# Rounded three-term products for four projections of a perceiver block, w_down loaded late, and a new order of work on every engine

## The chip, the cores and the metric

The kernel runs on one core of a Trainium2 chip. The metric is the device time of one execution in microseconds (us); lower is better. The core has four compute engines that run their own instruction streams and meet only through semaphores: PE (TensorE, matrix products into PSUM), DVE (VectorE), ACT (ScalarE) and POOL (GpSimd). SP (SyncE) issues most DMAs. Each engine works strictly in the order in which its instructions are written, so a wait at the head of a queue holds everything behind it.

## The reference, cut to what matters

One perceiver block on 64 sequences of 64 rows, 256 wide (4096 rows in all), with a context of 256 rows for each sequence:

```python
x = x + xattn(layernorm(x), ctx)      # 16 heads of 16, layernorm of q and k per head, softmax over 256
x = x + attn(layernorm(x))            # causal over 64 rows, extra term with tanh(q), J, tanh(k)
x = x + ffn(layernorm(x))
# in attn:  Q, K, V = n @ Wq.T + bq, n @ Wk.T + bk, n @ Wv.T + bv
# in ffn:   probs = softmax(h @ router_w); the two best of 16 experts (gate/up 256->128, down 128->256)
#           shared  = (silu(h @ shared_gate_w) * (h @ shared_up_w)) @ shared_down_w
```

Everything is f32. The products that the change touches are `n @ [Wq Wk]` (128 rows by 512 columns for each tile), `n @ Wv` (256 columns), `h @ router_w` (16 columns) and `h @ [shared_gate shared_up]` (512 columns), each with an inner size of 256, which is two blocks (KD = 2) of 128.

## The kernel before, in words

The rows are cut into 32 tiles of 128 (two sequences each). The tiles go through a software pipeline: in step s, an engine works on parts of tile s - lag, and the lag of each part is the number in its `on(s, odd, lag, part, ...)` call. Before the change the lags run from 0 to 6, so there are 32 + 6 steps (`LAGS = 6`, line 46), written out one after the other. The order of the parts within a step is written by hand for every engine in its own `step` function: PE from line 712, ACT from line 936, POOL from line 1056, DVE from line 1355, SP from line 417. PSUM banks are shared by lists of uses (`C_USES`, `B_USES`, `S_USES`, `O_USES`, lines 50 to 53): `claim` makes PE wait, before it writes a bank, until the bank's previous use in the list has been read. Ring C has one bank, ring B two (even and odd places of the list), S is the group of four banks used as one, O one bank.

What one step does on PE, with the names that the text uses:

- R0 and R1 (`rough_scores`, line 544): bf16 scores of the cross attention. DVE takes maxima of them (mx, line 1220), MT (`maxima_turned`, line 553) transposes the maxima, and DVE adds them to the query (`shifted`, line 1225).
- C0 and C1 (`scores`, line 565), then ACT's four exponentials (line 863), then PV0 to PV3 (`weighted`, line 582), DVE's `heads_out` (lines 1234 and 1237), X1 (`cross_output`, line 489 into oA), DVE's `cross_residual` (line 1244) and `self_stats` (lines 1141 to 1146), POOL's power (line 1005) and DVE's `self_normalised` (line 1150), which gives x1n.
- NT (transposes x1n, line 484), ACT's copy into x1T (line 815), QK (`self_qk`, x1T times wa_qk) and VP (`self_values`, x1T times wa_v), both by `product` at line 489. DVE's `self_split`, ACT's tanh, TQ and TK (line 608), MIX (line 617), SS (`self_scores`, lines 626 and 634), the softmax, PT0 and PT1 (`probs_turned`, line 649), O0 and O1 (line 663), WO (line 489 with wa_o).
- HT (transposes h), ACT's copy into hT, RT (`route`, hT times w_route), GU (`gate_and_up`, hT times ws_gu), ST, Y (`down`), and CNT (`counts`, lines 689 to 692), from which DVE's `rows_placed` works out where POOL's indirect DMAs scatter the rows (line 1053).
- K0, K1, V0, V1 (`context_product`, line 500): keys and values of the context. These are already three rounded (fp32r) terms: ct by wx_kv, ct by wx_kv_rest, ct_rest by wx_kv, where the rest is what rounding left out. DVE makes ct (`context_split`), POOL ct_rest (`context_rest`, line 1028). XT and Q make the query, KT and QT transpose keys and queries, and ACT copies those out with `keys_in` (two of 2048 columns, lines 877 and 879) and `queries_in`.

`product` issues one f32 matmul for each of the two blocks of 128; an f32 matmul has two MATMUL records in the trace, so an f32 product shows as x4.

After the pipeline the expert phase works through 80 slots of 128 rows: SP loads the rows that were scattered (from `load_slot`, once every scatter has landed and DVE has worked out the slots, `slots_known`), PE multiplies with w_gu (line 783) and w_down (line 799), and POOL scatters the results. Last, SP reads the two expert rows of each token into a ring of eight buffers (`yg`), DVE adds them to the stored base rows, and ACT writes the output. The weights of the experts, w_down among them, are loaded in twelve pieces of 512 KB in steps 6 to 17, and DVE halves w_down at the head of step 34 (line 1358).

## Time and profile before

| | |
|---|---|
| median of 3 runs | 1395.54 us (1392.45 to 1396.56) |
| the profiled execution, its own time | 1382.54 us |
| its span (first to last instruction) | 1380.7 us |
| PE busy | 1240.6 us, 90% of the span |
| DVE, ACT, POOL busy | 984.4, 698.1, 450.4 us |
| mean granted TensorE clock | 0.955 of full speed |
| chain that ended last | PE 82%, DVE 9%, issue 4%, DMA 2% |

The profiled execution ran 13 us below the median of the runs. In the page's 40 slices of 34.5 us, the first two are the fill, some 30 the steady pipeline, two its drain, and the last six the experts and the output. The end of a matmul record is modelled and overlaps the start of the next, so the distance from start to start tells what a group of matmuls costs.

### The profile page before, as it was taken

How to read it: one execution, taken by the hardware profiler on the slowest of the kernel's cores; microseconds unless marked ns; L12 is line 12 of the kernel's file. 1: busy time of each engine (PE TensorE's matmuls, PEld its weight loads, DVE VectorE, ACT ScalarE, POOL GpSimd, SP SyncE). 2: the span in 40 equal slices, each digit the busy share in tenths (PEclk: the TensorE clock that was granted, in tenths of full speed). 3: DMA queues.
4: the chain of work that ended last, by engine and by line, in shares of the span. 5: the costliest groups of instructions: out<-in, count | busy, mean ns of one | idle time of the engine just before them, and what ended most of it. 6: DMA issues, size and time to landing. Idle time of an engine off the chain costs nothing.

```text
span 1380.7 us, 54869 instructions
## 1 busy us (share of the span) xinstructions
PE 1240.6 (90%) x22808; PEld 1024.0 (74%) x22808; DVE 984.4 (71%) x2498; ACT 698.1 (51%) x1377; POOL 450.4 (33%) x436
## 2 busy tenths in 40 slices
PE   3789999999999999999999999999999986699950
PEld 3677878888888878788878787888888864488840
DVE  7458777777777777777777777777777763365547
ACT  1345555555555555555555555555555542255520
POOL 1322333333333333333333333333333222155530
PEclk7789999999999999999999999999999998699985
DMA  4100111111111111103111100111111002586558
GB/s 155 39 21 4 48 49 49 49 49 49 49 49 51 56 44 51 34 30 100 33 34 33 36 29 28 34 33 34 34 38 33 15 14 63 157 245 188 163 188 262
DMA packets 82579, 92.12 MB, mean 67 GB/s; under 512 B 17248, under 2 KB 72544, under 8 KB 82016
## 3 DMA queue, kind: packets, MB, share of 16 engines
q1 hardware_dynamic: 70816, 65.41, 16.4%
q0 software_dynamic: 6912, 19.01, 3.8%
q8 instruction: 185, 3.03, 0.9%
q10 hardware_dynamic: 4608, 4.20, 0.9%
q14 instruction: 58, 0.48, 0.1%
HBM read 61.19 MB, written 33.78 MB: 69 GB/s over the span
## 4 chain that ended last, share of the span: by engine, by line
PE 82%; DVE 9%; issue 4%; DMA 2%; ACT 1%; POOL 1%; SPq 0%; DVEq 0%; POOLq 0%; ACTq 0%
PE ringB L489 16%; PE ringC L500 14%; PE oA L582 10%; PE banksS L565 9%; DVE mx L1220 6%; PE banksS L783 5%; PE banksS L529 4%; PE ringB L663 3%; PE ringB L617 2%; PE ringB L649 2%; PE banksS L634 2%; PE ringB L484 2%; DMA out<-ksq 2%; PE oA L489 2%; PE banksS L544 2%
## 5 line engine op out<-in xcount | busy, mean ns | idle before, releaser
L863 ACT ACTIVATE pt<-banksS 128x1024 f32<-128x1024 f32 x128 | 127.7, 1023 | 129.6 <-PE banksS L565 118.0
L1039 POOL TENSOR_TENSOR kn<-kc,rr 128x512 f32<-128x512 f32 x64 | 66.6, 1062 | 336.0 <-DVE rr L1208 336.0
L500 PE MATMUL ringC<-wx_kv,ct 128*128 128x256 f32 x512 | 159.9, 312 | 13.6 <-DVE ws_down L1362 6.2
L1220 DVE TENSOR_REDUCE mx<-banksS 128x8 f32<-128x2048 f32 x64 | 146.3, 2287 | 0.9 <-PE banksS L544 0.9
L500 PE MATMUL ringC<-wx_kv_rest,ct 128*128 128x256 f32 x512 | 146.8, 287 | 0.0
L500 PE MATMUL ringC<-wx_kv,ct_rest 128*128 128x256 f32 x512 | 146.0, 285 | 0.0
L1033 POOL TENSOR_TENSOR sc<-sc,rz 128x1024 f32<-128x1024 f32 x32 | 62.3, 1948 | 223.5 <-DVE rz L1281 223.5
L565 PE MATMUL banksS<-qT,kT 17*128 17x64 f32 x4096 | 132.4, 278 | 0.9 <-DVE qT L1225 0.9
L565 PEld LDWEIGHTS banksS<-qT,kT 17*128 17x128 f32 x4096 | 123.5, 191 | 7.9 <-issue 1.4
L500 PEld LDWEIGHTS ringC<-wx_kv,ct 128*128 128x128 f32 x512 | 99.3, 194 | 27.6 <-DVE pos_u L1338 7.8
L1234 DVE RECIPROCAL rz<-oA 128x128 f32<-128x128 f32 x64 | 61.3, 957 | 55.5 <-PE oA L582 55.5
L500 PEld LDWEIGHTS ringC<-wx_kv_rest,ct 128*128 128x128 f32 x512 | 99.5, 194 | 0.1
L500 PEld LDWEIGHTS ringC<-wx_kv,ct_rest 128*128 128x128 f32 x512 | 99.4, 194 | 0.0
L1076 POOL DMA_INDIRECT expert_rows<-kc,row_to x80 | 76.5, 956 | 68.1 <-DVE kc L1469 65.2
L582 PEld LDWEIGHTS oA<-pt,va 128*32 128x32 f32 x4096 | 65.3, 111 | 41.8 <-issue 37.3
L877 ACT ACTIVATE kT<-banksS,cols 128x2048 bf16<-128x2048 f32 x32 | 65.8, 2057 | 58.2 <-PE banksS L529 58.2
L582 PE MATMUL oA<-pt,head_ones 128*32 128x64 f32 x4096 | 87.2, 222 | 3.8 <-issue 3.7
L582 PE MATMUL oA<-pt,va 128*32 128x64 f32 x4096 | 87.2, 225 | 3.1 <-ACT pt L863 2.5
L783 PE MATMUL banksS<-w_gu,qk 128*128 x320 | 84.4, 387 | 0.0
L1028 POOL TENSOR_TENSOR ct_rest<-ct_in,ct 128x1024 fp32r<-128x1024 f32 x32 | 76.3, 2385 | 7.8 <-DVE ct L1102 7.0
L1266 DVE TENSOR_REDUCE mx<-banksS 128x16 f32<-128x1024 f32 x32 | 39.2, 1224 | 50.9 <-PE banksS L634 50.9
L582 PEld LDWEIGHTS oA<-pt,head_ones 128*32 128x32 f32 x4096 | 70.8, 112 | 6.2 <-issue 5.8
(219 smaller groups left out, 2957.0 us busy)
## 6 DMA issues: line engine op xcount, KB each, us to landing
ct_in<-in_ctxT SPq DMA_DIRECT2D x64, 256.0 KB, 3.1
...
```

The source lines that it names most:

```text
L489: mm = pe.matmul(bank_[:, 0:n], lhs(k), rhs[:, k, 0:n], start=(k == 0), stop=(k == 1))
L500: mm = pe.matmul(ringC[:, half * DIM:(half + 1) * DIM], left[:, p, k, j // 2, (j % 2) * P:(j % 2 + 1) * P], right[:, k, part * DIM:(part + ...
L565: mm = pe.matmul(banksS[:, i, at:at + N], kT[lo:hi, q4, b * M + mc * P:b * M + (mc + 1) * P], qT[lo:hi, q4, b * N:(b + 1) * N], start=True ...
L582: mm = pe.matmul(oA[32 * p4:32 * p4 + 32, at:at + N], left, pt[:, g, 2 * (p4 % 2) + odd, p4 // 2, mc, :], start=(odd == 0 and mc == 0), st ...
L783: mm = pe.matmul(bank(2 + s % 2)[:, 0:2 * F], xgT[:, s % 2, k * P:(k + 1) * P], w_gu[:, k, :, :].rearrange("p e f -> p (e f)")[:, bass.ds( ...
L863: act.activation(pt[:, g, :, :, :, :].rearrange("p i q c n -> p i (q c n)"), banksS[:, :, g * 256:(g + 1) * 256], ACT.Exp)\
L877: act.activation(kT16[:, :, :].rearrange("p q m -> p (q m)"), banksS[:, :, :].rearrange("p q m -> p (q m)"), ACT.Identity, bias=cols[:, 3: ...
L1028: pool.tensor_tensor(ct_rest[:, p, :, :, :], ct_in[:, :, :, :], ct[:, p, :, :, :].bitcast(F32), ALU.subtract).then_inc(ev["ct_rest_ready"] ...
L1033: pool.tensor_tensor(pn[:, :, :], ex[:, :, :], rz2[:, :].unsqueeze(2).to_broadcast([P, 2 * HP, N]), ALU.mult).then_inc(ev["pn_ready"].sem, 1)
L1039: pool.tensor_tensor(kn[:, 2 * jj:2 * jj + 2, :, 0:HD].rearrange("p j h d -> p (j h) d"), kc[:, 2 * jj:2 * jj + 2, :].rearrange("p j (h d) ...
L1076: pool.indirect_dma_start(out=y_d[:, :], out_offset=bass.IndirectOffsetOnAxis(ap=row_to[:, j:j + 1], axis=0), in_=y[:, c, :], in_offset=No ...
L1220: dve.tensor_reduce(mx[:, 2 * r:2 * r + 2, :, HD].rearrange("p q i -> p i q"), banksS[:, :, :].rearrange("p i (q m) -> p i q m", q=2), AX. ...
```

## The change

1. wa_qk, wa_v, w_route and ws_gu are kept as a rounded part and a rest (fp32r), and so are x1T and hT. QK, VP, RT and GU are made by a new function, `split_product`: left by right, left by right's rest (four matmuls), then, after a second wait, left's rest by right (two matmuls). ACT's copies now write the rounded part and count as the first of two events; DVE gets two new parts, `self_rows_rest` and `ffn_rows_rest`, which subtract the rounded part from PSUM and give the second.
2. The raw weights are loaded into sc, qkn and qk4, and DVE splits them at the head of step 3 (four copies, four subtractions). It used to wait for them at the head of step 2.
3. w_down shares its memory with kn and kT, so its four pieces are loaded after C1 of the last tile (SP waits for it behind step 34), and DVE halves it at the head of step 36 and not 34. The other eight pieces go out in steps 6 to 13.
4. The output phase takes other free buffers for its ring of eight and for the stored base rows.
5. `LAGS` is 7. The orders of PE, ACT, POOL and DVE, and the lists of bank uses, are new; some parts have another lag (K0 1 to 2, PT1 4 to 5, `values` 1 2 to 3, `context_split` 0 to 1, `cross_biased` and `cross_rstd` 2 to 1, `self_normalised` 3 to 4, `row_copied` 5 to 6, the scatters 5 and 6 to 6 and 7). SP asks for the rows before the context.

```diff
-LAGS = 6
+LAGS = 7
 LEAD = 8
-C_USES = (("K1", 2), ("XT", 2), ("Q", 2), ("V0", 2), ("CNT", 5), ("V1", 2), ("K0", 1))
-B_USES = (("NT", 4), ("O0", 5), ("O1", 5), ("WO", 5), ("QK", 4), ("TQ", 4), ("TK", 4), ("HT", 5), ("MIX", 4), ("RT", 5), ("GU", 5), ("ST", 5), ("VP", 4), ("Y", 5), ("PT0", 4), ("PT1", 4))
+C_USES = (("K0", 2), ("K1", 2), ("XT", 2), ("Q", 2), ("V0", 2), ("CNT", 5), ("V1", 2))
+B_USES = (("NT", 4), ("PT1", 5), ("O0", 5), ("O1", 5), ("QK", 4), ("WO", 5), ("TQ", 4), ("TK", 4), ("HT", 5), ("RT", 5), ("GU", 5), ("MIX", 4), ("VP", 4), ("ST", 5), ("Y", 5), ("PT0", 4))
 S_USES = (("R0", 3), ("R1", 3), ("C0", 3), ("C1", 3), ("SS", 4), ("KT", 2))
 O_USES = (("MT", 3), ("PV0", 3), ("PV1", 3), ("X1", 3), ("QT", 2))
...
+kn_kT = sb("kn_kT", [P, 2, 2048])
+kn = kn_kT[:, 0, :].rearrange("p (j h d) -> p j h d", j=4, h=H)
 wx_kv_in = kc[:, :, :].rearrange("p (k a) n -> p k (a n)", k=KD)
-kT = sb("kT", [P, QG, 2 * M])
+kT = kn_kT[:, 1, :].rearrange("p (g m) -> p g m", g=QG)
+w_down = kn_kT[:, :, :].rearrange("p a (e d) -> p (a e) d", d=DIM)
...
+rounded = {}
+for u in ("NT", "HT"):
+    rounded[u], free[u] = Event(free[u].sem, 1, 2), Event(free[u].sem, 2, 2)
...
             load_self_weights()
-        if 6 <= s < 18:
-            load_expert_weights(s - 6)
+        if 6 <= s < 14:
+            load_expert_weights(s - 2)
         if s == 20:
             sp.dma_start(rows_d[E * ROOM:E * ROOM + E * P, :], w["dump_rows"]).then_inc(pads_out, 16)
+        if s != 1:
+            on(s, odd, 1, load_rows)
         if s != 0:
             on(s, odd, 0, load_context)
-        if s != 1:
-            on(s, odd, 1, load_rows)
         on(s, odd, 5, row_numbers)
...
     for s in range(TILES + LAGS):
         step(s, s % 2)
+        if s == TILES + 2:
+            sp.wait_ge(full["C1"].sem, full["C1"].of(TILES - 1))
+            for piece in range(4):
+                load_expert_weights(piece)
     def load_slot(j):
         c = j % DEEP
...
+    def split_product(bank_, u, t, left, left_rest, source, right, right_rest, n):
+        pe.wait_ge(rounded[source].sem, rounded[source].of(t))
+        for r in (right, right_rest):
+            for k in range(KD):
+                pe.matmul(bank_[:, 0:n], left[:, k, :], r[:, k, 0:n], start=(r is right and k == 0), stop=False)
+        pe.wait_ge(free[source].sem, free[source].of(t))
+        for k in range(KD):
+            mm = pe.matmul(bank_[:, 0:n], left_rest[:, k, :], right[:, k, 0:n], start=False, stop=(k == 1))
         mm.then_inc(full[u].sem, 1)
...
+            pe.wait_ge(weights_set, 2)
         claim(pe, B_USES, B_BANKS, "QK", b)
-        pe.wait_ge(free["NT"].sem, free["NT"].of(b))
-        product(bankB("QK"), "QK", lambda k: x1T[:, k, :], wa_qk, 2 * DIM)
+        split_product(bankB("QK"), "QK", b, x1T, x1T_rest, "NT", wa_qk, wa_qk_rest, 2 * DIM)
     def heads_turned(b, p, u, side):
...
         pe.wait_ge(free["NT"].sem, free["NT"].of(b))
-        product(bankB("VP"), "VP", lambda k: x1T[:, k, :], wa_v)
+        split_product(bankB("VP"), "VP", b, x1T, x1T_rest, "NT", wa_v, wa_v_rest, DIM)
     def probs_turned(b, p, g):
...
     def step(s, odd):
         on(s, odd, 3, rough_scores, 0)
         on(s, odd, 4, self_rows_turned)
+        on(s, odd, 5, probs_turned, 1)
+        if s != 2:
+            on(s, odd, 2, context_product, "K0", 0, 0)
+        on(s, odd, 3, rough_scores, 1)
         on(s, odd, 5, self_weighted, 0)
         on(s, odd, 5, self_weighted, 1)
         on(s, odd, 2, context_product, "K1", 1, 0)
+        on(s, odd, 4, self_qk)
         on(s, odd, 5, self_output)
-        on(s, odd, 4, self_qk)
+        on(s, odd, 3, maxima_turned)
         on(s, odd, 2, rows_turned)
-        on(s, odd, 3, rough_scores, 1)
-        on(s, odd, 2, query_product)
         on(s, odd, 4, heads_turned, "TQ", 0)
         on(s, odd, 4, heads_turned, "TK", 1)
-        on(s, odd, 3, maxima_turned)
+        on(s, odd, 2, query_product)
         on(s, odd, 5, ffn_rows_turned)
-        on(s, odd, 4, self_mix)
         on(s, odd, 3, scores, 0)
         on(s, odd, 5, route)
...
         on(s, odd, 3, scores, 1)
         on(s, odd, 3, weighted, 1)
         on(s, odd, 2, context_product, "V0", 0, 1)
+        on(s, odd, 4, self_scores)
+        on(s, odd, 4, self_values)
+        on(s, odd, 3, weighted, 2)
+        on(s, odd, 3, weighted, 3)
         on(s, odd, 5, gated_turned)
-        on(s, odd, 4, self_scores)
-        on(s, odd, 3, weighted, 2)
-        on(s, odd, 4, self_values)
-        on(s, odd, 3, weighted, 3)
         on(s, odd, 2, keys_turned)
+        on(s, odd, 5, down)
         on(s, odd, 3, cross_output)
+        on(s, odd, 2, queries_turned)
         if s != TILES - 1 + 5:
             on(s, odd, 5, counts)
-        on(s, odd, 5, down)
+        on(s, odd, 4, probs_turned, 0)
         on(s, odd, 2, context_product, "V1", 1, 1)
-        on(s, odd, 4, probs_turned, 0)
-        on(s, odd, 2, queries_turned)
-        on(s, odd, 4, probs_turned, 1)
-        if s != 1:
-            on(s, odd, 1, context_product, "K0", 0, 0)
...
     def step(s, odd):
+        on(s, odd, 3, values, 1)
+        on(s, odd, 4, self_rows_in)
         on(s, odd, 5, probs_in, 1)
-        on(s, odd, 4, self_rows_in)
+        on(s, odd, 5, outputs_in, 0)
         on(s, odd, 5, outputs_in, 1)
-        on(s, odd, 5, outputs_in, 0)
+        on(s, odd, 4, self_tanh)
+        on(s, odd, 2, query_rows_in)
+        on(s, odd, 4, heads_in, "TQ", 0)
         on(s, odd, 2, squares, 1)
-        on(s, odd, 2, query_rows_in)
-        on(s, odd, 4, self_tanh)
         on(s, odd, 2, squares, 0)
-        on(s, odd, 4, heads_in, "TQ", 0)
         on(s, odd, 4, heads_in, "TK", 1)
-        on(s, odd, 5, row_copied)
         on(s, odd, 5, ffn_rows_in)
-        on(s, odd, 4, mixed_in)
         on(s, odd, 2, query_squares)
+        on(s, odd, 6, row_copied)
         on(s, odd, 3, exponential, 0)
         on(s, odd, 3, exponential, 1)
+        if s != TILES - 1 + 5:
+            on(s, odd, 5, routing_exponential)
+        on(s, odd, 4, mixed_in)
         if s == TILES - 1 + 5:
             on(s, odd, 5, routing_exponential)
         on(s, odd, 5, gate_tanh)
-        if s != TILES - 1 + 5:
-            on(s, odd, 5, routing_exponential)
         on(s, odd, 3, exponential, 2)
         on(s, odd, 3, exponential, 3)
-        on(s, odd, 5, gated_rows_in)
         on(s, odd, 2, values, 0)
         on(s, odd, 4, self_values_in)
         on(s, odd, 4, self_exponential)
+        on(s, odd, 5, gated_rows_in)
         on(s, odd, 2, keys_in)
-        on(s, odd, 2, values, 1)
         on(s, odd, 2, queries_in)
         on(s, odd, 4, probs_in, 0)
...
     def step(s, odd):
-        on(s, odd, 2, cross_biased)
-        on(s, odd, 2, cross_rstd)
+        on(s, odd, 7, rows_scattered, 1)
         on(s, odd, 5, ffn_rstd)
+        on(s, odd, 2, keys_scaled, 1)
         on(s, odd, 4, self_biased)
-        on(s, odd, 2, keys_scaled, 1)
-        on(s, odd, 2, keys_scaled, 0)
-        on(s, odd, 6, rows_scattered, 1)
         if s != 1:
             on(s, odd, 1, context_rest)
+        on(s, odd, 2, keys_scaled, 0)
         on(s, odd, 4, self_probs)
+        on(s, odd, 6, rows_scattered, 0)
+        on(s, odd, 1, cross_biased)
         on(s, odd, 3, self_rstd)
-        on(s, odd, 5, rows_scattered, 0)
+        on(s, odd, 1, cross_rstd)
     context_rest(0, 0)
     pool.wait_ge(weights_set, 1)
...
+    def self_rows_rest(b, p):
+        dve.wait_ge(rounded["NT"].sem, rounded["NT"].of(b))
+        freed(dve, full["QK"], b)
+        freed(dve, full["VP"], b)
+        dve.tensor_tensor(x1T_rest[:, :, :].rearrange("p k n -> p (k n)"), bankB("NT")[:, 0:DIM],
+                          x1T[:, :, :].rearrange("p k n -> p (k n)").bitcast(F32), ALU.subtract).then_inc(free["NT"].sem, 1)
...
     def step(s, odd):
-        if s == TILES + 2:
+        if s == TILES + 4:
             dve.wait_ge(expert_weights_in, 16 * 12)
             dve.tensor_scalar(w_down[:, :, :], w_down[:, :, :], 0.5, None, ALU.mult).then_inc(weights_set, 1)
-        if s == 2:
+        if s == 3:
             dve.wait_ge(self_weights_in, 16 * 7)
+            split = ((wa_qk, wa_qk_rest, wa_qk_in), (wa_v, wa_v_rest, wa_v_in), (ws_gu, ws_gu_rest, ws_gu_in), (w_route, w_route_rest, w_route_in))
+            for whole, _, source in split:
+                ins = dve.tensor_copy(whole[:, :, :], source)
+            ins.then_inc(setup_dve, 1)
+            dve.wait_ge(setup_dve, 9)
+            for whole, rest, source in split:
+                dve.tensor_tensor(rest[:, :, :], source, whole[:, :, :].bitcast(F32), ALU.subtract)
             dve.tensor_scalar(jmix[:, :, :], jmix[:, :, :], cols[:, 4:5], None, ALU.mult)
             dve.tensor_scalar(ws_down[:, :, :], ws_down[:, :, :], 0.5, None, ALU.mult).then_inc(weights_set, 1)
+        on(s, odd, 4, self_normalised)
+        on(s, odd, 3, maxima, 0)
+        on(s, odd, 4, self_rows_rest)
+        on(s, odd, 2, cross_normalised)
         on(s, odd, 2, keys, 0)
-        on(s, odd, 3, maxima, 0)
-        on(s, odd, 2, cross_normalised)
+        on(s, odd, 3, maxima, 1)
         on(s, odd, 2, keys, 1)
+        on(s, odd, 4, self_split)
         on(s, odd, 5, self_residual)
         on(s, odd, 5, ffn_stats)
-        on(s, odd, 4, self_split)
-        on(s, odd, 3, maxima, 1)
+        on(s, odd, 3, shifted)
         on(s, odd, 5, ffn_normalised)
-        on(s, odd, 3, shifted)
+        on(s, odd, 2, queries)
+        if s != 1:
+            on(s, odd, 1, context_split)
+        on(s, odd, 5, ffn_rows_rest)
         on(s, odd, 2, key_sums, 1)
-        on(s, odd, 2, queries)
-        on(s, odd, 2, key_sums, 0)
         on(s, odd, 2, query_sums)
         on(s, odd, 5, routing_logits)
+        on(s, odd, 2, key_sums, 0)
         on(s, odd, 2, inverse_sigmas)
...
         on(s, odd, 2, queries_scaled)
-        if s not in (TILES - 1 + 4, TILES - 1 + 5):
-            on(s, odd, 5, rows_placed)
         if s != TILES - 1 + 5:
             on(s, odd, 5, rows_without_experts)
         on(s, odd, 3, cross_residual)
+        on(s, odd, 1, cross_stats)
+        if s not in (TILES - 1 + 4, TILES - 1 + 5):
+            on(s, odd, 5, rows_placed)
         on(s, odd, 3, self_stats)
-        on(s, odd, 1, cross_stats)
-        on(s, odd, 3, self_normalised)
-        if s != 0:
-            on(s, odd, 0, context_split)
     for s in range(TILES + LAGS):
         step(s, s % 2)
```

The diff leaves out the views of the shared buffers, the loads of the raw weights, and unchanged lines of the orders.

## Rows read from the trace of the kernel before

**Rows 1.** Windows: us of the stretch, then PE, PEld, DVE, ACT, POOL busy, granted clock, DMA

```profile
253.50:288.10 34.60, 33.99 (x709) 28.19 (x712) 26.87 (x68) 19.69 (x34) 11.59 (x11) 1.00 0.17 49
```

**Rows 2.** Timeline of PE: start and duration in us; R0 starts, and one steady step

```profile
46.71 0.42 PE L544 MATMUL banksS<-kT,qT 16*64 16x256 bf16 x16
...
252.77 0.42 PE L544 MATMUL banksS<-kT,qT 16*64 16x256 bf16 x16
...
254.69 0.38 PE L500 MATMUL ringC<-wx_kv,ct 128*128 128x256 f32 x1
...
256.21 1.03 PE L489 MATMUL ringB<-wa_o,o2T 128*128 128x256 f32 x4
257.07 1.88 PE L489 MATMUL ringB<-wa_qk,x1T 128*128 128x512 f32 x4
258.79 0.38 PE L484 MATMUL ringC<-ident,xn 128*128 128x128 f32 x2
...
265.65 0.62 PE L489 MATMUL ringB<-w_route,hT 128*128 128x16 f32 x4
266.12 1.96 PE L489 MATMUL ringB<-ws_gu,hT 128*128 128x512 f32 x4
268.01 0.66 PE L582 MATMUL oA<-pt,va 128*32 128x64 f32 x32
...
276.49 1.13 PE L489 MATMUL ringB<-wa_v,x1T 128*128 128x256 f32 x4
277.56 0.66 PE L582 MATMUL oA<-pt,va 128*32 128x64 f32 x32
...
287.03 0.42 PE L544 MATMUL banksS<-kT,qT 16*64 16x256 bf16 x16
...
1112.34 0.42 PE L544 MATMUL banksS<-kT,qT 16*64 16x256 bf16 x16 [1.19 <-ACT qT L871]
```

**Rows 3.** Waits: who waited for whom, us in total, times, longest

```profile
PE oA L553 <- DVE mx L1220: 10.1, 32, 1.2
...
PE ringC L489 <- ACT xnT L815: 9.5, 32, 1.7
...
PEld ringB L663 <- ACT pT L914: 7.9, 31, 1.1
```

**Rows 4.** Groups of DVE instructions: busy us, mean ns of one, idle before

```profile
L1220 DVE TENSOR_REDUCE mx<-banksS 128x8 f32<-128x2048 f32 x64 | 146.3, 2287 | 0.9 <-PE banksS L544 0.9
...
L1353 DVE TENSOR_TENSOR base<-ringB,x 128x256 f32<-128x256 f32 x32 | 13.5, 423 | 8.2 <-PE ringB L489 8.2
```

**Rows 5.** Timelines of DVE, then POOL, late in a steady step: start, duration in us

```profile
730.51 0.42 DVE L1244 TENSOR_TENSOR x<-oA,xres 128x256 f32<-128x256 f32 x1
...
731.64 0.15 DVE L1146 TENSOR_SCALAR lnB<-lnB 128x1 f32<-128x1 f32 x1
...
728.82 1.96 POOL L1033 TENSOR_TENSOR sc<-sc,rz 128x1024 f32<-128x1024 f32 x1 [6.33 <-DVE rz L1281]
731.88 0.57 POOL L1005 TENSOR_TENSOR lnB<-lnB,minushalf 128x1 f32<-128x1 f32 x1 [1.10 <-DVE lnB L1146]
732.64 1.06 POOL L1053 DMA_INDIRECT rows_by_expert<-h,pos_u  x1 [0.20 <-issue]
733.73 0.76 POOL L1024 TENSOR_TENSOR xres<-xt,rows 128x256 f32<-128x256 f32 x1
```

**Rows 6.** Timelines of POOL, ACT and DVE: step 2 of the fill, end of the drain

```profile
36.68 2.35 POOL L1028 TENSOR_TENSOR ct_rest<-ct_in,ct 128x1024 fp32r<-128x1024 f32 x1
...
1189.42 0.37 ACT L815 COPY suT<-ringB 128x256 f32<-128x256 f32 x1 [1.56 <-PE ringB L484]
...
1192.15 0.06 DVE L1442 MEMSET top<- 128x1 f32 x1
```

**Rows 7.** DMA issues: KB each where known, median us from issue to landing

```profile
w_down<-in_e_down SPq DMA_DIRECT2D x4, 512.0 KB, 4.1
...
rows_by_expert<-h,pos_u POOLq DMA_INDIRECT x64, 2.8
```

54 lines of the change are left out of this document (32 added, 22 removed).

## The prediction

> **What bounds the kernel now.** I read the windows view first, cut by steps of the pipeline: in a steady step of 34.6 us PE is busy 33.99, DVE 26.87, ACT 19.69, POOL 11.59, at the full granted clock and with the DMA engines 17% busy [rows 1]. PE is full and every other engine has 7 us or more to spare. Then I read PE's timeline. R0 opens each step: tile 0's stands at 46.71 and tile 31's at 1112.34, so 31 steps take 1065.6 us, 34.37 each, and the one at 252.77 takes 34.26 [rows 2]. This stretch is three quarters of the time, so a change of 0.1 us in a step is worth 3.1 us. Last I read the waits: PE's largest repeated ones are short, 0.32 us a step for the second maxima (10.1 / 32), 0.30 for xnT (9.5 / 32) and 0.25 for pT (7.9 / 31) [rows 3]. So the reader should see a PE-bound loop with under 2 us of gaps in each step: time comes from less PE work or from fewer gaps, and a new gap costs its whole length.
>
> **Products, per tile.** From start to start QK takes 258.79 - 257.07 = 1.72 us, GU 1.89, RT 0.47 and VP 1.07 [rows 2]. QK is two f32 matmuls of 512 columns; if each runs as four passes, a pass takes 1.72 / 8 = 0.215 us. A context product is twelve fp32r matmuls of 256 columns in 1.52 us (254.69 to 256.21), 0.127 each with its start [rows 2]. The change issues six fp32r matmuls in each product. No row shows one with 512 columns. The lower bound is one pass, 0.215, the upper twice the 256-wide one, 0.254; I take 0.215, because part of the 0.127 is the start of a group and the weight load, which 512 columns hide. So QK and GU take 1.29 each: -0.43 and -0.60 (GU's row holds some 0.17 of waiting, which a later place removes). VP goes to 6 x 0.127 = 0.76, -0.31. RT has 16 columns and is bound by its weight loads: four records took 0.47, six at 0.117 to 0.127 take 0.70 to 0.76, +0.29. Together **-1.05 us a step**.
>
> **What the rests cost.** DVE gets two subtractions of 256 columns from PSUM, 0.42 us each by the like sum at line 1353 [rows 4]: 0.85 us of the 7.7 that DVE has free [rows 1], so nothing by load. By place: QK now waits for ACT's copy and then DVE's subtraction, but PT1, K0, R1, O0, O1 and K1 stand between NT and QK, over 4 us, and the subtraction comes right behind the first maxima, 2.8 us into the step. Behind that new wait on DVE stand xn, the first keys and the second maxima; ACT's copy is done long before. RT waits for hT's rest, and C0 (2 us) covers it. If those covers went, PE would wait for the 0.42 and the copy, under 1 us for each product.
>
> **Waits that go and come.** The new order puts WO and QK ahead of MT, TQ and TK ahead of Q, and NT and PT1 apart from O0: the three waits above go, -0.87 [rows 3]. New ones, by walking the new queues:
> - R1 needs the first maxima, 2.29 us [rows 4] behind R0. Only NT, PT1 and K0 are between (two small transposings and 1.5 us): 0.3 late.
> - QT now follows X1 directly and takes its bank, so it waits for `cross_residual`, 0.42 us [rows 5] and two handoffs: 0.65 late.
> - V1 takes the bank of CNT, so it waits for `rows_placed`, four small instructions. The nearest rows, the sum and the three small ones of the statistics, go from 730.51 to 731.79, 1.28 us [rows 5]; these are smaller, so 0.9. PT0 is four transposes, half of WO's 0.86 [rows 2], and covers 0.43: 0.48 late.
> - TQ behind tanh: 0.05.
>
> That is +1.48; between nothing, if another engine runs earlier than I walked, and 2, if all the handoffs are worse. The sum is -1.05 - 0.87 + 1.48 = -0.44 a step; the old step also has gaps under 0.1 us that I did not find in the new one, and the whole walk gives 33.7 to 33.9 for 34.26. I take **-0.5, times 31: -15.5 us**.
>
> **Fill.** In step 2 POOL now makes ct_rest of tile 1 between the two halves of kn, and KT waits for both: +2.35 [rows 6]. ACT's `values` moves behind `queries_in`, two copies of about 0.3 us (like the 0.37 of suT's [rows 6]) off the way to the first R0: -0.6. DVE's split of the weights is four copies and four subtractions, some 4000 columns in and out, about 5 us from the 0.42 for 256 columns with its fixed part [rows 4]; it stands at the head of step 3, where DVE waits for R0 in any case, while PE does KT and ACT copies the keys. Cover gone, it would cost up to 5 once. Fill: +1.7.
>
> **Drain and end.** SP issues w_down's four pieces (512 KB, 4.1 us to land in the old place [rows 7]) behind the stored base of step 34. Even one after the other they need 17 us, and DVE wants them at the head of step 36, some 20 us later, where it next waits for WO; the halving is hidden there too. A late landing would push everything behind it one for one. Leaving the steady part gives nothing, as the DMA engines were idle. The last row copy is now in ACT's step 37, behind the copy of suT, which ended at 1189.8; the copy (0.4), the scatter (1.06 [rows 5]) and its landing (2.8 [rows 7]) end at 1194.1, where DVE had told the slots at 1192.2 [rows 6] and SP needs both: +2.0. The other reordering in the drain I take as zero, within 3 either way. The expert and output phases only change buffers: zero.
>
> **Sum:** -15.5 + 1.7 + 2.0 = -11.8 us against the profiled 1382.5, so 1370.7 there. The median of the runs stands 13 us above the profiled execution; against it, 1395.5 - 11.8 = **1383.7 us**. About 0.3% (4.2 us) is what a measurement of this kernel can tell from no change.
>
> **Rivals.**
> 1. *The new gaps are half of what I walked* (chance 0.17). For it: DVE and ACT have 7 and 15 us free [rows 1], so a little earlier on either closes a gap; against it: each gap is a chain of PE, DVE and back with no slack inside. -1.2 a step, -37 + 4: 1362 us.
> 2. *A 512-wide fp32r matmul costs twice the 256-wide* (0.13). Then QK and GU take 1.52, +0.46 a step: the steady gain is gone, and with the fill and the end it comes to 1395 to 1399. For it: the only fp32r rows are at 0.127 for 256; against it: f32 passes of 512 columns run at 0.215 [rows 2].
> 3. *Slower: POOL's queue at the end of the step* (0.10). In the new order POOL must do `self_probs` (1.96), a scatter (1.06) with 0.2 ahead of it and `cross_biased` (0.76) before `self_rstd` [rows 5]; before, the scatter and cross_biased came after it. I walk `self_rstd` as asked for about 0.2 to 0.3 us after POOL is free. x1n, NT and the copy for QK hang on it, and DVE's first instruction of the step now waits there, with the maxima behind it. Once POOL is more than 0.3 us later than I have it, NT moves; 0.9 later eats the whole gain. With a scatter that takes twice its 1.06, NT is 0.8 late: +0.3 a step, +9 and +4: 1408 us. For it: nothing in that queue can overtake; against it: 1.06 is steady.
> 4. *The clock falls* (0.02). The granted clock is 1.00, its 2.4 GHz level, in the steady window although PE stops briefly in every step [rows 1, 3]; the new order has as many stops. If a tenth of the matrix work ran at the lower level, 1.2 GHz, at half speed, a step would gain 3.4 us, over 100 us in all: about 1490. The Trainium skill, TensorE: Matmul & The Clock Gate, section "A second HAM failure mode: psum-queue depth-cycling", tells of short idle times between groups of matmuls that made the clock go to and fro. By that rule the old kernel should show it already; this trace, with 1.00, doesn't agree.
>
> That the products aren't the bound is no rival: PE is full.
>
> **How the numbers follow.** The forecast has 0.58. Its own range is 1370 to 1393: the sum of new gaps between 1.1 and 1.7, and 3 us of drain. The whole range, 1356 to 1399, takes in most of rivals 1 and 2; what is left out is the rest of 1, and 3 and 4. Faster by over 0.3%: 0.54 of the forecast and all of rival 1, 0.71. Within 0.3%: 0.04 and most of rival 2, 0.15. Slower: rivals 3 and 4 and the rest, 0.14.
>
> **What the new profile would show.** R0 to R0 in the steady part at 33.9 or a little less (33.2 for rival 1, 34.3 for 2, 34.6 for 3); QK and GU 1.3 us from start to start, RT 0.7 to 0.76, VP 0.7 to 0.76; PE waiting for line 1244 before QT, for line 1338 before V1, for line 1220 before R1, and no more for xnT; DVE near 27.7 a step; NT not waiting for more than 0.2; the first R0 near 48.5; DVE not waiting for w_down; the first slot's rows a little later behind the last R0 than now. QK waiting for a rest inside the product, or PE idle for POOL's line 1005 through x1n, would prove me wrong, and so would a period under 33.

## The result, and the profile after

The changed kernel takes 1458.47 us (median of 4, 1454.78 to 1462.31) beside 1395.81 for the kernel before: a ratio of 1.0454 with a 95% interval of 1.0422 to 1.0486. I had forecast 1383.7, faster. It is slower by 4.5%, outside my range. Executions of one kernel can be fast or slow, and ratios compare fast ones alone, each with runs of the kernel before taken beside them; only e4 has slow ones, two of its four and its trace among them, and its two fast ones took 1504.7 us in the mean.

The page of the profiled execution: span, busy times, the row of the granted clock, and the chain that ended last.

```profile
span 1457.0 us, 55516 instructions
PE 1262.4 (87%) x23064; PEld 1073.7 (74%) x23064; DVE 1067.5 (73%) x2570; ACT 692.7 (48%) x1377; POOL 451.0 (31%) x436
PEclk7679999999999999999999999999999997599985
PE 68%; DVE 13%; issue 10%; DMA 3%; POOL 2%; ACT 1%; SPq 1%; another core or an unknown queue 0%; DVEq 0%; POOLq 0%; ACTq 0%
```

PE's share of the chain fell from 82% to 68%, DVE's and "issue" rose: PE now stops. The timeline of after, one step of PE that answers to [rows 2], and then the last R0, the drain's SP and POOL, and the first slot:

```profile
228.56 0.42 PE L569 MATMUL banksS<-kT,qT 16*64 16x256 bf16 x16
229.19 0.60 PE L674 MATMUL ringB<-ident,sc 128*128 128x128 f32 x4
229.54 0.37 PE L525 MATMUL ringC<-wx_kv,ct 128*128 128x256 f32 x1
231.87 0.42 PE L569 MATMUL banksS<-kT,qT 16*64 16x256 bf16 x16 [0.65 <-DVE mx L1243]
234.80 0.63 PE L511 MATMUL ringB<-wa_qk,x1T 128*128 128x512 f32 x2
236.21 1.03 PE L503 MATMUL ringB<-wa_o,o2T 128*128 128x256 f32 x4
242.21 0.39 PE L511 MATMUL ringB<-w_route,hT 128*128 128x16 f32 x2
242.90 0.71 PE L511 MATMUL ringB<-ws_gu,hT 128*128 128x512 f32 x2
243.45 0.98 PE L511 MATMUL ringB<-ws_gu_rest,hT 128*128 128x512 f32 x2
244.22 1.05 PE L514 MATMUL ringB<-ws_gu,hT_rest 128*128 128x512 f32 x2
245.21 1.08 PE L607 MATMUL oA<-pt,va 128*32 128x64 f32 x32
...
261.27 0.66 PE L545 MATMUL oA<-ident,qn 128*128 128x128 f32 x4 [0.52 <-DVE x L1267]
263.20 0.39 PE L525 MATMUL ringC<-wx_kv,ct 128*128 128x256 f32 x1 [0.28 <-DVE filled_to L1356]
264.82 0.42 PE L569 MATMUL banksS<-kT,qT 16*64 16x256 bf16 x16
...
1171.04 0.42 PE L569 MATMUL banksS<-kT,qT 16*64 16x256 bf16 x16
1213.16 29.89 SPq L413 DMA_DIRECT2D h<-in_row_number  x2
1244.04 15.72 SPq L421 DMA_DIRECT2D rows_by_expert<-in_pad_rows  x16
1264.06 1.19 POOL L1076 DMA_INDIRECT rows_by_expert<-h,pos_u  x1 [14.32 <-DMA rows_by_expert<-in_pad_rows]
1270.71 0.66 PE L798 MATMUL banksS<-ident,pt 128*128 128x128 f32 x2 [10.41 <-DMA pt<-rows_by_expert]
```

R0 to R0 is 36.26 here against 34.26 in [rows 2]. R1 starts 2.33 us after K0 (229.54 to 231.87), where K0 alone takes 1.54. QK takes 236.21 - 234.80 = 1.41. From 243.45 on, GU and PV0 take about twice the time they should (PV0's first half is 1.08 here for 0.65 elsewhere). The windows view of after says why: that step, the stretch before GU, the stretch of GU and PV0, and the whole steady part, with the granted clock in the column PEclk.

```profile
core 0: us, PE busy (x) PEld busy (x) DVE busy (x) ACT busy (x) POOL busy (x), PEclk, DMA share, GB/s
228.56:264.80 36.24, 34.69 (x699) 29.81 (x698) 28.27 (x69) 19.26 (x34) 11.55 (x12) 0.95 0.17 46
241.40:243.40 2.00, 2.00 (x40) 1.89 (x37) 1.21 (x5) 1.22 (x3) 0.00 (x0) 1.00 0.03 8
243.50:246.90 3.40, 3.40 (x69) 2.55 (x67) 2.96 (x13) 0.89 (x2) 0.00 (x0) 0.50 0.00 0
120.00:1171.04 1051.04, 988.80 (x20258) 847.72 (x20259) 842.30 (x1968) 563.08 (x960) 331.05 (x317) 0.98 0.12 37
```

For 3.4 us the clock is at its 1.2 GHz level. This "fall" comes in 13 of the 28 middle steps; the kernel before has none. All 13 begin at RT or GU, 14.1 to 15.2 us into the step, and in the 4 us before each of them PE is idle for at most 0.09 us: none follows a stop of PE. Steps without a fall take 35.88 us, with one 36.60, all 36.21; before it was 34.38 throughout. I use these three numbers (clean, fallen, mean) for every kernel.

The waits view of after, rows that answer to [rows 3]:

```profile
PE banksS L569 <- DVE mx L1243: 21.1, 30, 2.3
PE oA L545 <- DVE x L1267: 16.3, 31, 0.7
PE oA L607 <- DVE oT L1260: 5.7, 15, 0.4
```

xnT, pT and the second maxima have left the list as forecast. The first maxima stand in it with 0.70 a step, QT's bank with 0.53. The third row is new too: PV2 takes the bank that DVE's `heads_out` (oT) still reads. It stands in 15 steps, just those without a fall; there VP, with this wait behind it, takes 1.32, and in the fallen steps 0.90. For PE's idle time as a whole, the windows view of before, from tile 2's R0 to tile 31's:

```profile
115.00:1112.34 997.34, 973.31 (x20002) 806.57 (x20000) 772.36 (x1909) 566.02 (x958) 331.99 (x315) 1.00 0.14 41
```

PE's time outside matmuls is 24.0 us here and 62.2 in the steady row of after, 0.8 and 2.1 us a step.

**Where the 76.3 us of span went.** The first R0 stands at 50.13 for 46.71: +3.4. From it to the last R0: 1120.9 for 1065.6, +55.3. From the last R0 to the end: 286.0 for 268.4, +17.6.

### The profile page after: what moved, and what is told of

Its sections match the earlier page's. It is cut to its first block, busy times and chain, and to the rows that moved or that the text cites. A ratio compares the mean times of both kernels' runs of the same rounds, so it can differ in the third digit from the quotient of the medians.

```text
span 1457.0 us, 55516 instructions
## 1 busy us (share of the span) xinstructions
PE 1262.4 (87%) x23064; PEld 1073.7 (74%) x23064; DVE 1067.5 (73%) x2570; ACT 692.7 (48%) x1377; POOL 451.0 (31%) x436
## 4 chain that ended last, share of the span: by engine, by line
PE 68%; DVE 13%; issue 10%; DMA 3%; POOL 2%; ACT 1%; SPq 1%; another core or an unknown queue 0%; DVEq 0%; POOLq 0%; ACTq 0%
PE ringC L525 9%; PE oA L607 8%; PE banksS L590 6%; PE ringB L511 6%; PE banksS L806 5%; DVE mx L1243 5%; PE banksS L554 4%; PE ringB L503 3%; PE ringB L514 3%; PE banksS L569 3%; PE ringB L642 2%; PE ringB L633 2%; PE ringB L688 2%; DMA out<-ksq 2%; PE ringC L503 2%
## 5 line engine op out<-in xcount | busy, mean ns | idle before, releaser
L1062 POOL TENSOR_TENSOR kn_kT<-kc,rr 128x512 f32<-128x512 f32 x64 | 68.3, 1067 | 298.0 <-DVE rr L1231 298.0
L1056 POOL TENSOR_TENSOR sc<-sc,rz 128x1024 f32<-128x1024 f32 x32 | 62.4, 1950 | 259.0 <-DVE rz L1304 259.0
L590 PE MATMUL banksS<-qT,kn_kT 17*128 17x64 f32 x4096 | 131.1, 276 | 0.0
L590 PEld LDWEIGHTS banksS<-qT,kn_kT 17*128 17x128 f32 x4096 | 122.2, 189 | 9.6 <-issue 5.9
L1028 POOL TENSOR_TENSOR lnC<-lnC,minushalf 128x1 f32<-128x1 f32 x32 | 18.2, 567 | 274.9 <-DVE lnC L1169 274.9
L607 PEld LDWEIGHTS oA<-pt,va 128*32 128x32 f32 x4096 | 69.5, 116 | 35.4 <-issue 22.4
L1346 DVE TENSOR_SCALAR hot<-numbers,best_no 128x16 bf16<-128x16 f32 x64 | 77.1, 1248 | 1.1
```

The costliest lines, as they stand in the source:

```text
L590: mm = pe.matmul(banksS[:, i, at:at + N], kT[lo:hi, q4, b * M + mc * P:b * M + (mc + 1) * P], qT[lo:hi, q4, b * N:(b + 1) * N], start=True ...
L607: mm = pe.matmul(oA[32 * p4:32 * p4 + 32, at:at + N], left, pt[:, g, 2 * (p4 % 2) + odd, p4 // 2, mc, :], start=(odd == 0 and mc == 0), st ...
L1062: pool.tensor_tensor(kn[:, 2 * jj:2 * jj + 2, :, 0:HD].rearrange("p j h d -> p (j h) d"), kc[:, 2 * jj:2 * jj + 2, :].rearrange("p j (h d) ...
L1346: ins = dve.tensor_scalar(hot16[:, k, :], expert_no, best_no[:, k:k + 1], None, ALU.is_equal)
```

## The experiments

**e1: POOL's order.** The line-by-form view showed that DVE's `hot` took 1248 ns for 452 before, while POOL ran ct_rest. POOL: `self_biased`, `context_rest`, then both halves of `keys_scaled`.

```diff
-on(s, odd, 2, keys_scaled, 1)
 on(s, odd, 4, self_biased)
 on(s, odd, 1, context_rest)
+on(s, odd, 2, keys_scaled, 1)
```

> Only POOL's order is changed: x1b and ct_rest of the next tile are made ahead of the two halves of kn, not between them, so that no long POOL instruction runs while DVE makes hot (line 1346). Theory A (POOL and DVE block each other there: hot has a mean of 1248 ns after the change and 452 before): hot's mean falls to under 600 ns, DVE's busy time falls by 40 to 50 us, and as hot stands ahead of heads_out on DVE, the steady step falls from 36.2 us by 1 to 1.6, about 1420 us in all. Theory B (the fall of TensorE's clock behind C0 and RT in about half of the steps is the loss): hot gets short, but the time stays within 10 us of 1457. Theory C (the new waits that were forecast, before QT, V1 and R1, are the loss): the same as B, within 10 us.

1459.32 us, 1.0465 (1.0428 to 1.0502). The groups of DVE by form, after and then e1:

```profile
L1346 DVE TENSOR_SCALAR hot<-numbers,best_no 128x16 bf16<-128x16 f32 x64 | 77.1, 1248 | 1.1
```

```profile
L1346 DVE TENSOR_SCALAR hot<-numbers,best_no 128x16 bf16<-128x16 f32 x64 | 13.2, 250 | 1.1
```

The block is gone, 64 us of DVE with it, and the time is the same. It was not the cause. A clean step is a little shorter (35.50), but 16 steps fall for 13, and the mean step is 36.39.

**e2: MIX ahead of C0 again** (PE, ACT and the list of banks).

> MIX is put back ahead of C0 on PE (with its place in the list of bank uses), and ACT's copy of it ahead of the exponentials; the rest is the changed kernel. Theory B (the granted clock falls because the stretch HT, C0, RT has little in the array, and a full product ahead of it would keep it up): granted clock back to 1.00 in the steady windows, where 13 of 29 windows of 36 us had 0.95, and 15 to 25 us less: about 1436. Theory A (DVE blocked by POOL) and C (waits): no change within 8 us, whatever the clock does, since PE then waits longer for DVE.

1469.67 us, 1.0546 (1.0515 to 1.0578). 11 of 28 steps still fall, and a step is 36.79; PE now also waits 0.4 us ahead of MIX for ACT's copy of qk. So with RT split, MIX's place is not what lets the clock fall. With RT plain it was not tried.

**e3: plain f32 products in the new orders.** x1T and hT are whole, so the two rests are zero and unused.

> The four products are plain f32 again (two f32 matmuls each), in the new order; the copies and the two subtractions (now of zero) are kept. If the products alone are worth what their durations say (QK 1.41 for 1.72, GU 1.55 for 1.72, VP 0.8 for 0.86, RT 0.69 for 0.47, together 0.36 us a step), PE-bound: +11 us, about 1469. If the step is set by the chain over DVE and POOL (theory A), the products hide behind it: within 5 us of 1458. If the clock's fall hangs on the six short matmuls of RT (a form of theory B), the clock recovers and the time falls by 10 to 20 us.

1462.65 us, 1.0477 (1.043 to 1.0524). QK, GU, RT and VP have their old times back, 10 steps fall, the mean step is 36.46, and the kernel is as slow: 4 us more than after where the durations promised 11. The products are not the loss.

**e4: the orders, lags and bank lists of before, with the split products**, x1T's rest behind the first maxima.

> The products in three rounded terms, the late w_down and the split of the weights are kept, but the orders of all engines, the lags and the lists of bank uses are those of before, with the two subtractions put in at the places where DVE has time (behind the first maxima, behind the first key sums). If the new orders are the whole loss (theories A, B and C alike): faster than the kernel before by the products, 0.4 to 0.8 us a step: 1370 to 1385 us. If the three-term products or their subtractions are the loss: 1420 us or more.

1516.09 us (1494.24 to 1519.66), 1.0801 (1.0705 to 1.0896), the slowest of all. Timeline of e4, PE at O1:

```profile
707.91 1.08 PE L688 MATMUL ringB<-pT,v 64*32 64x64 f32 x32 [1.94 <-DVE x1T_rest L1382]
708.92 0.58 PE L525 MATMUL ringC<-wx_kv,ct 128*128 128x256 f32 x1
```

O1 takes NT's bank, which is free only when DVE has read it for the rest, behind 2.3 us of maxima. All 28 steps fall in this trace (38.68).

**e5: three moves against the three waits of the new order.** PE's part; ACT's copy for PT0 and DVE's `rows_placed` move with it.

```diff
-on(s, odd, 3, rough_scores, 1)
 on(s, odd, 5, self_weighted, 0)
 on(s, odd, 5, self_weighted, 1)
+on(s, odd, 3, rough_scores, 1)
...
+on(s, odd, 5, counts)
 on(s, odd, 3, cross_output)
-on(s, odd, 2, queries_turned)
-on(s, odd, 5, counts)
 on(s, odd, 4, probs_turned, 0)
+on(s, odd, 2, queries_turned)
```

> The new order with three moves: R1 behind O0 and O1 on PE; CNT ahead of X1 and PT0 between X1 and QT on PE; rows_placed ahead of cross_residual on DVE (ACT's two copies follow PE). Theory A (the waits that the order brought are the loss: R1 0.75, QT 0.67, V1 0.48 us a step, and the falls of the granted clock, 0.7 a step, follow from PE's stops): a step of 34.3 with the falls and 33.6 without, 1400 or 1378 us. Theory B (the two rests hold banks and DVE, and every order pays): a step of 35.8 or more, the waits come back before other slots, over 1445. If the falls stay while the three waits are gone, the stops at these places don't cause them.

1490.87 us, 1.0705 (1.067 to 1.0739), step 37.45 (clean 36.29). Timeline of e5, three engines:

```profile
228.18 0.42 PE L569 MATMUL banksS<-kT,qT 16*64 16x256 bf16 x16 [1.08 <-ACT qT L894]
231.31 0.41 DVE L1382 TENSOR_TENSOR x1T_rest<-ringB,x1T 128x256 fp32r<-128x256 f32 x1
231.78 1.02 PE L688 MATMUL ringB<-pT,v 64*32 64x64 f32 x64 [0.94 <-DVE x1T_rest L1382]
```

Each wait came back as another: R0 waits for qT, which QT's later place made late, and O0, now ahead of R1, waits for NT's bank. Both theories got their waits wrong; the head of the step is one chain through DVE's first maxima.

**e6 and e8: no split at all, no rests, in the old and in the new orders.** Together with e7 and after they are a square. What e6 keeps of the change is the late w_down, the layout and the splitting of the weights.

> The orders of before, the four products plain f32 as before, no rests at all; what stays of the change: w_down loaded in the drain, the new buffers, the split of the weights at step 3 (its results unused). Theories A and B: 1393 to 1403 us, a step of 34.4 at the full granted clock, and only the end differs. Theory C (the late w_down and the new layout of SBUF cost): a step over 34.7 or a drain over 10 us longer, 1405 to 1420.

> The new order, the four products plain f32, no rests: with the kernel above that has the old orders and no split, the two differ by the orders alone, and from the kernel after by products and rests alone. Theory A: the waits stay, a step of 36 to 36.5, 1455 to 1465 us. Theory B (holds and DVE's two subtractions): 34.5 or less, under 1405.

e6 took 1393.85 us, 1.0004 (0.9986 to 1.0022): the late w_down, the layout and the splitting of the weights cost nothing. e8 took 1462.48 us, 1.0516 (1.0486 to 1.0547). **The orders alone cost 5.1%**, more than the whole change. Windows view of the steady parts, e6 and then e8:

```profile
120.64:1121.50 1000.86, 977.41 (x20001) 806.92 (x20000) 769.99 (x1908) 566.16 (x958) 331.91 (x315) 1.00 0.13 38
```

```profile
120.55:1172.63 1052.08, 994.80 (x20012) 805.59 (x20012) 822.24 (x1909) 560.69 (x957) 329.52 (x314) 0.99 0.12 36
```

The same instructions; PE's time outside matmuls is 23.5 us in e6 and 57.3 in e8. Clean steps take 34.51 and 35.95, and 7 of e8's 28 fall, 6 of them at RT or GU although RT is plain there.

**e7: as e4, the rest of x1T ahead of the first maxima.**

> The orders of before, split products, the rest of x1T ahead of the first maxima on DVE and the rest of hT behind the second half of key_sums. With the rest behind the maxima this kernel took 1516 us. Bank hold (NT's bank, which O1 takes, is free only when DVE has made the rest): O1 waits 0.5 to 1.0 instead of 1.94, a step of 34.5 to 35.5, 1395 to 1430. If it stays over 1480, the hold is not what cost the 120 us. If the products alone count, 1365 to 1375.

1409.08 us, 1.0107 (1.0079 to 1.0135). One part moved on DVE, 96 us less than the 1504.7 of e4. O0 and O1 take 1.59 for 1.13; 8 steps fall, all at RT or GU (two of them again in PV1), and take 36.80 for 34.49.

**e9: K1 ahead of O0, to cover the hold of the bank.**

> Old orders, split products, the rest ahead of the first maxima (1409 us, a step of 35.16), and K1 ahead of O0 and O1 on PE, so that the 1.5 us of K1 stand before the product that takes NT's bank. Bank hold: O1's wait of 0.35 to 0.5 goes, a step of 34.7; if the falls of the clock to 1.2 GHz (in 11 of 30 steps there, at GU) came from that stop they go too, and the step is 34.0 to 34.2: 1375 to 1385 us, faster than the kernel before. If the falls come from the shape of RT's products they stay: 34.6 to 34.8, 1393 to 1400.

1422.31 us, 1.0253 (1.0216 to 1.0291): a miss. Timeline of e9:

```profile
228.67 1.10 PE L503 MATMUL ringB<-wa_o,o2T 128*128 128x256 f32 x4 [0.60 <-ACT o2T L943]
```

K1 had been the cover of WO. The falls at GU stayed (9 steps).

**e10: e9 with RT plain f32 again, from a full copy of hT.**

> The kernel above with one product set back: RT is four plain f32 matmuls of 16 columns (0.47 us) from a full copy of hT that ACT makes as well (0.37 us more on ACT); QK, GU and VP stay split. If RT's six short matmuls bring the falls of the clock, they go: granted 1.00 in nearly all steps, a step of 33.8 to 34.1, 1368 to 1380 us. If they stay in a third of the steps, RT is not what brings them, and it gains 0.2 a step, 6 us.

1398.23 us, 1.0078 (1.0054 to 1.0102): 24 us less than e9. Only 2 of 28 steps fall. RT's own 0.22 a step is 7 us of it; the rest went with the falls.

**e11: no split, RT twice.**

```diff
+pe.wait_ge(free["HT"].sem, free["HT"].of(d))
+for k in range(KD):
+    pe.matmul(bankB("RT")[:, 0:E], hT[:, k, :], w_route[:, k, 0:E], start=(k == 0), stop=(k == 1))
 split_product(bankB("RT"), "RT", ...)
```

(`split_product` is the plain f32 pair here.)

> The old orders without any split (1394 us, the clock 1.00 in every step) and RT's four f32 matmuls issued twice, the same result written again: a stretch of short matmuls of 0.94 us in place of 0.47 ahead of GU. If a longer stretch of 16-column matmuls between C0 and GU is what lets the clock fall, many steps show 0.95 and GU 1.9 to 3.6: a step over 35.4, over 1425 us. If not, the clock stays at 1.00 and the step grows by 0.47 at most: 1400 to 1409 us.

1441.78 us, 1.0382 (1.0331 to 1.0432). Windows view of e11, the two RTs, and GU behind them:

```profile
202.48:203.40 0.92, 0.92 (x13) 0.92 (x9) 0.00 (x0) 0.78 (x1) 0.00 (x0) 1.00 0.00 0
203.80:207.20 3.40, 3.40 (x44) 1.52 (x46) 3.02 (x14) 1.25 (x3) 0.02 (x1) 0.57 0.00 0
```

Half of the steps fall (37.28); the clean ones take 34.99, which is e6's 34.51 and the 0.45 of the second RT. PE doesn't stop here: it is busy throughout both stretches.

**e12: the pad rows ahead of the last row numbers on SP.**

```diff
-on(s, odd, 5, row_numbers)
+if s != TILES - 1 + 5:
+    on(s, odd, 5, row_numbers)
 if s == TILES - 1 + 5:
     pad_experts()
+    on(s, odd, 5, row_numbers)
```

> The kernel after, with one swap on SP in step 36: the sixteen pad rows before the row numbers of tile 31, which wait for a scatter that the seventh lag put a step later. If that wait holds the pads, and the pads the last scatters, the pads go out near 1233 to 1236 in place of 1244 and the first slot's rows come 5 to 8 us sooner: 1450 to 1454 us. If the last row copy or the last Y bounds the end, under 2 us are gained.

1454.27 us, 1.0453 (1.0412 to 1.0493). Timeline of e12, SP:

```profile
1236.15 16.23 SPq L421 DMA_DIRECT2D rows_by_expert<-in_pad_rows  x16
1264.71 4.28 SPq L464 DMA_DIRECT2D pt<-rows_by_expert  x5
```

From the last R0 (1173.78 here) the pads go out 62.4 us later for 73.0, and the end comes 278.6 later for 286.0: 7.4 us less of the drain. The mean step of this execution was 36.36, so the total shows 4 us of it.

**e13: both causes removed.** Old orders; RT plain; ACT copies x1T and hT whole out of PSUM, which frees the bank as before, and DVE makes both parts from SBUF.

```diff
+dve.tensor_copy(whole, full_rows).then_inc(rounded[u].sem, 1)
...
+dve.tensor_tensor(whole_rest, full_rows, whole.bitcast(F32), ALU.subtract).then_inc(rests[u].sem, 1)
```

> Old orders; QK, GU and VP split, RT plain f32; ACT copies x1T and hT whole out of PSUM as before, and DVE makes the rounded part and the rest from that copy in SBUF, so NT's and HT's banks are free as early as in the kernel before (hold theory: no more wait of O1), and RT stays short (clock theory: few falls). Against 1394 us and 34.5 a step without any split: QK -0.31, GU -0.32, VP -0.17, so 33.7 a step and 1366 to 1374 us, faster than the kernel before by 1.3% or more. If DVE's four more instructions make the maxima or xn late, 34.2 to 34.5: 1385 to 1394. If falls still come in a third of the steps, 34.3: 1388.

**1379.77 us** (1374.45 to 1390.84), 0.9903 (0.9867 to 0.994): 1% faster than the kernel before, and faster than the one after. Its steady part in the windows view:

```profile
118.85:1103.41 984.56, 955.63 (x20174) 834.61 (x20174) 799.77 (x2024) 568.30 (x958) 332.33 (x315) 0.99 0.13 39
```

A clean step takes 33.74, as the two theories (the held bank and RT's products) say, although PV2 and PV3 take 0.2 more than in e6. Two steps still fall, so the mean is 33.95, 0.2 or some 6 us of steady part, and from the last R0 to the end it takes 275.8 for e6's 270.6. Together that is more than the 6 us by which it misses the expected range. O0 and O1 are at 1.09. RT plain and the freed banks were not measured apart in this kernel.

**e14: no split, old orders, R1 behind O1.**

> Old orders, no split (1394 us, clock 1.00 in every step), R1 moved from behind XT to behind O1 on PE, so that PE stops for the first maxima near the head of the step as in the new order: a wait of 0.9 to 1.1 us, 0.3 of R1's old wait gone. If stops of PE alone bring the falls of the clock at GU, many steps show 0.95 and the step is over 35.8: over 1435 us. If they don't, the clock stays at 1.00 and the step is 34.9 to 35.4: 1408 to 1422 us.

1478.56 us, 1.061 (1.0585 to 1.0635). **e16: the same, and PE's stop filled** with matmuls whose results are not used.

```diff
+if bb == 1:
+    for _ in range(8):
+        pe.matmul(bankB(u)[:, 0:DIM], wx_kv_rest[:, 0, 0:P], wx_kv[:, 0, 0:DIM], start=True, stop=True)
```

> The kernel with R1 behind O1 (1478 us, a step of 37.24, where PE stops 1.1 us for the first maxima and K1 and WO then run at half the clock in most steps), with eight fp32r matmuls of 256 columns, 1.0 us, whose results nobody uses, written into O1's bank ahead of O1. R1 can't start sooner, so PE only works where it stood. If the stop is what brings the clock down, the falls go although PE does more: K1 1.54 and WO 0.86 again, a step of 36.0 to 36.3, 1437 to 1450 us. If K1 and WO are slow for another reason, nothing is gained: 1478 or more.

1449.69 us, 1.0418 (1.0373 to 1.0463): 29 us less, with 8 matmuls more in each step. Windows view from R0 to R1 and behind R1, e14 and then e16:

```profile
196.88:200.29 3.41, 2.45 (x100) 1.53 (x99) 3.21 (x3) 1.47 (x5) 0.68 (x2) 1.00 0.16 50
200.30:203.70 3.40, 3.40 (x24) 3.13 (x17) 0.69 (x1) 0.35 (x1) 0.00 (x0) 0.62 0.00 0
```

```profile
232.55:236.01 3.46, 3.46 (x107) 2.53 (x107) 3.21 (x3) 1.24 (x5) 0.68 (x2) 1.00 0.13 45
236.01:240.10 4.09, 4.09 (x28) 3.01 (x21) 1.88 (x6) 0.86 (x3) 0.12 (x1) 1.00 0.00 0
```

In e14 PE is idle for 0.96 us ahead of R1's end, and K1 and WO then run at the low level; 22 of 28 steps fall. In e16 none does. The clean steps are equal, 36.19 and 36.20: the filler costs nothing, and the falls were the whole difference. What stays, 1.7 over e6, is the wait for the maxima, and XT, 0.99 for 0.31.

**e15: the repairs of e13 in the new orders.**

> The new orders with the same two repairs (rests from SBUF, RT plain f32). Order theory (the new waits cost most, about 1.6 us a step, whatever the products): a step of 35.4 to 35.7, 1432 to 1444 us, still 3% slower than the kernel before. Product theory (holds and RT are what cost): under 34.5, under 1405.

1452.67 us, 1.0408 (1.0382 to 1.0434), a step of 36.23: 6 us less than after. The loss is the orders'. RT is plain here, and 12 steps fall all the same, 9 of them at GU.

**e17: the control for e11.**

> The control for the doubled RT (1442 us): old orders, no split, RT once, and GU's first f32 matmul of 512 columns issued once more ahead of GU, 0.43 to 0.45 us, about what the second RT took. If the 16-column matmuls are what lets the clock fall, it stays at 1.00 here and the step grows by 0.43: 1404 to 1410 us. If any added work at this place does it, 1430 to 1445.

1452.21 us, 1.045 (1.0404 to 1.0497). Timeline of e17:

```profile
243.32 1.10 PE L715 MATMUL ringB<-ws_gu,hT 128*128 128x512 f32 x2
244.26 1.88 PE L507 MATMUL ringB<-ws_gu,hT 128*128 128x512 f32 x4
250.66 0.47 PE L600 MATMUL oA<-pt,head_ones 128*32 128x64 f32 x17 [0.43 <-issue]
```

My size was wrong: one f32 matmul of 512 columns takes 0.94, not 0.43. On the clock it answers: 3 of 28 steps fall for e11's 14, with twice the added time, and those 3 begin in PV1 behind stops of 0.3 to 0.4 us, none at RT or GU. But the clean step is 36.35, 1.84 over e6: GU explains 0.86, PV3 grew by 0.4, and PV1 from 1.17 to 2.00, with stops in the middle of its matmuls that nothing in the profile releases ("issue"). So time alone, against e11, would mislead; the step and the clock must be read apart.

| kernel | us | ratio | clean, fallen (steps), mean step |
|---|---|---|---|
| before | 1395.8 | 1 | 34.38, none |
| after | 1458.5 | 1.0454 | 35.88, 36.60 (13), 36.21 |
| e6 old orders, no split | 1393.9 | 1.0004 | 34.51, none |
| e8 new orders, no split | 1462.5 | 1.0516 | 35.95, 37.48 (7), 36.33 |
| e7 old orders, split | 1409.1 | 1.0107 | 34.49, 36.80 (8), 35.15 |
| e13 old orders, split, repaired | 1379.8 | 0.9903 | 33.74, 36.72 (2), 33.95 |
| e15 new orders, split, repaired | 1452.7 | 1.0408 | 35.66, 36.98 (12), 36.23 |

## Why the prediction was wrong

**The step that failed is the walk of the new queues** ("+1.48" of waits and "the whole walk gives 33.7 to 33.9"). The mean step is 36.21 for 34.38: +1.83 where I had -0.5. The walk counted the new waits of single parts and took everything else as unchanged. No single term makes the miss of 2.3; the largest, 0.69, is one that I put at nothing without a reason. Term by term, in distances from start to start:

| term | forecast | measured |
|---|---|---|
| QK, GU, VP, RT (full clock) | -0.43, -0.60, -0.31, +0.29 | -0.31, -0.32, -0.17, +0.22 |
| waits of before gone | -0.87 | -1.07 |
| R1 for the first maxima | +0.30 | +0.78 |
| QT, V1 | +0.65, +0.48 | +0.67, +0.48 |
| PV2 for DVE's `heads_out` (15 steps) | 0 | +0.22 |
| falls of the clock | 0 | +0.33 |
| short pieces next to others (XT, Q, HT, MIX, ST, QT, V1) | 0 | +0.69 |
| not assigned | | +0.3 |

- **Right:** that PE is the bound, that the three old waits go, and QT's and V1's new waits with their sizes. e5 shows why the right sizes were not a right judgement: moved singly, these waits came back.
- **The products.** In the clean steps VP with the wait behind it is not 0.17 shorter but 0.25 longer than before. e8, where the products are plain, doesn't have this wait. So the new orders turn a part of what the products save into waiting, which is why e3 and e8 are hardly slower than after.
- **R1.** The maxima take the 2.29 us of [rows 4], but DVE begins them 0.96 us behind R0's start (0.72 before), so they end at 3.25 and not at the 2.8 that I walked. Another error is one of kind, and it costs this kernel nothing by itself: I asked if QK waits for the rest ("QK now waits for ACT's copy and then DVE's subtraction ... over 4 us"), and it doesn't. I did not ask who waits for the bank that the rest reads. e4, e5 and e7 show that wait: 1.94, 0.94 and about 0.46 us. In the kernel after, O0 stands behind R1's wait and is covered by it.
- **Rival 2 came half true.** QK's six matmuls take 1.41, 0.235 each, between my 0.215 and 0.254. With GU, which kept the 0.16 that a later place was to remove, and VP it costs 0.54 a step, and RT gave 0.07 back. e3 and e8 against after show that it is not what decided.
- **Rival 4, the clock, had 0.02.** I judged it by the clock of the kernel before, which never fell, and by "the new order has as many stops"; PE's time outside matmuls is 2.1 us a step for 0.8. e14 against e16 shows that a stop brings a fall (22 falls, none when filled), and e9 against e10 and e6 against e11 that RT's 16-column matmuls do in the old orders, with PE busy all the while. The Trainium skill, TensorE: Matmul & The Clock Gate, section "A second HAM failure mode: psum-queue depth-cycling", says that short idle times between groups of matmuls make the clock oscillate. For e14 and e16 the trace agrees, 0.62 and 1.00 behind R1; I had held the old kernel's 1.00 against it. It would not have given e11, where nothing is idle.
- **Which falls the kernel after has.** Those of the second kind: all 13 begin at RT or GU with PE busy, and none behind the stop for R1 (0.7 us). In e5, where the stop at the head is 1.2 to 1.3 us, 11 of 21 falls follow it. RT's split alone doesn't bring the 13: with RT plain, 9 of e3's 10 falls, 6 of e8's 7 and 9 of e15's 12 begin there too, and e6, with the old orders, has none. What in the new orders brings them is not shown. MIX, which used to stand between HT and C0, is the nearest difference, and it was put back (e2) only with RT split.
- **What a fall costs.** GU takes 2.54 for 1.57 and PV0 1.53 for 1.03, 1.5 us together; the step as a whole is only 0.72 longer, since the wait behind VP (0.42) is then gone and PV2 and PV3 are 0.2 shorter. So the 0.33 of the table is what is left of some 0.7.
- **Rival 3**, the slower one: x1n does wait 0.79 us a step for POOL's power (25.4 us in 32 times), but NT starts 0.37 behind R0 (228.93), directly after it, so PE doesn't wait. The end of POOL's queue was not tried by itself.
- **Not considered: DVE's `hot` beside POOL's ct_rest**, 1248 ns for 452. The Trainium skill, SBUF — State Buffer, section "SBUF: two separate sides", says that VectorE and GpSimd share a pair of ports, and that an instruction of either can hold it to its end; of VectorE's, those in a two-port mode or with two inputs in SBUF. Whether `hot` is one of these no run shows, but the times agree: 1.38 us in the mean for the 56 that run beside ct_rest and kn, 0.23 for those beside an idle POOL. e1 shows that it cost DVE's spare time only.
- **Fill:** +1.7 forecast, +3.4 measured. KT does wait for kn behind ct_rest, as I had it, but it starts 4.15 later (40.92 for 36.77) and not 2.35: ct_rest takes 2.78 there, and POOL begins kn 1.2 later, since DVE now makes ct before the sums that kn needs. The gain for `values` came: from KT's start to R0 it is 9.2 for 9.9.
- **Drain:** +2.0 forecast, +17.6 measured, and e8 has 14.7 more than e6 there, so it is the orders'. I took "the other reordering in the drain as zero". The seventh lag puts the scatter of tile 29 a step later; the row numbers of tile 31 wait for it on SP, the sixteen pads stand behind them, and the last scatters behind the pads. e12 took back 7.4. I had followed the last row copy and not SP's queue. w_down's late load is free (e6), as forecast.
